# Attention's PSUM banks shared out anew: four for maxima and two for scores, in place of three and three

## The reference, cut to what matters

```
q = (x @ wq_w.T + wq_b).reshape(b, t, H, HD)
k = (x @ wk_w.T + wk_b).reshape(b, t, HKV, HD)
v = (x @ wv_w.T + wv_b).reshape(b, t, HKV, HD)
k1 = k[:, :, 0, :]
v1 = v[:, :, 0, :]
scores = jnp.einsum('bqhd,bkd->bhqk', q, k1) / jnp.sqrt(jnp.float32(HD))
causal = jnp.tril(jnp.ones((t, t), dtype=bool))
scores = jnp.where(causal, scores, -jnp.inf)
weights = jax.nn.softmax(scores, axis=-1)
attn = jnp.einsum('bhqk,bkd->bqhd', weights, v1)
attn = attn.reshape(b, t, H * HD)
return attn @ wo_w.T + wo_b
...
x = _layernorm(x + _L3_attn_ref(x, ...), axis=-1)
```

## Time and profile before

| what | value |
|---|---|
| three executions | 1298.91, 1307.59 and 1310.77 us (median 1307.59) |
| the profiled execution | 1303.14 us, its span 1301.4 us |
| mean granted tensor-engine clock | 0.988 |
| PE busy | 1228.7 us, 94% of the span |
| DVE busy | 719.8 us, 55% |
| ACT busy | 439.8 us, 34% |
| POOL busy | 162.2 us, 12% |
| maxima's reductions on DVE (L2427) | 304, 186.4 us, mean 656 ns |
| exponentials on ACT (L2334) | 288, 156.9 us, mean 603 ns |

### The profile page before, as it was taken

How to read it: one execution, slowest core, us unless ns; L and a number is a source line. 1 busy time by engine, 2 the same in 40 slices (tenths; PEclk the granted TensorE clock), 3 DMA queues, 4 the chain that set the end, 5 groups by cost and what they waited for, 6 DMA issues and landing times. The chain is left out here.

```text
span 1301.4 us, 14425 instructions
## 1 busy us (share of the span) xinstructions
PE 1228.7 (94%) x5396; PEld 846.3 (65%) x5396; DVE 719.8 (55%) x1194; ACT 439.8 (34%) x751; POOL 162.2 (12%) x215
## 2 busy tenths in 40 slices
PE   7899999998998999998889999999999988999998
PEld 4788688644876788876565445455455534788886
DVE  4422565576657656453355678677767734443344
ACT  2121422212211114222333223666565566222221
POOL 0000000000086201002112110011011224000000
PEclk9999999999999999998999999999999998999999
DMA  8110023423045561004000010000000001022001
GB/s 346 33 49 16 33 97 131 169 97 146 1 146 194 206 229 26 22 1 138 1 1 1 5 44 1 2 2 1 2 2 2 3 2 49 25 73 73 1 25 41
DMA packets 18265, 79.07 MB, mean 61 GB/s; under 512 B 3104, under 2 KB 3872, under 8 KB 16032
## 3 DMA queue, kind: packets, MB, share of 16 engines
q1 hardware_dynamic: 18208, 78.32, 16.6%
HBM read 75.95 MB, written 2.10 MB: 60 GB/s over the span
## 5 line engine op out<-in xcount | busy, mean ns | idle before, releaser
L2427 DVE TENSOR_REDUCE mqa_top<-psum 128x1 f32<-128x512 f32 (+3 forms) x304 | 186.4, 656 | 50.6 <-PE psum L2219 25.0
L2334 ACT ACTIVATE mqa_prob<-psum 128x512 f32<-128x512 f32 x288 | 156.9, 603 | 85.2 <-PE psum L2249 81.2
L612 PE MATMUL psum<-L_ffn_x,L_ffn_w_up 128*128 128x512 f32 x624 | 143.8, 391 | 8.7 <-DVE L_ffn_hidden L767 7.7
L612 PEld LDWEIGHTS psum<-L_ffn_x,L_ffn_w_up 128*128 128x128 f32 x624 | 116.5, 188 | 36.0 <-DVE L_ffn_hidden L767 10.2
L612 PE MATMUL psum<-L_attn_x,L_attn_w_up 128*128 128x512 f32 x456 | 105.4, 393 | 3.9 <-DVE L_attn_hidden L767 3.9
L612 PEld LDWEIGHTS psum<-L_attn_x,L_attn_w_up 128*128 128x128 f32 x456 | 86.6, 190 | 22.5 <-issue 4.3
L2249 PE MATMUL psum<-mqa_stack_back,mqa_keys 100*128 100x512 f32 x208 | 96.3, 463 | 0.9 <-DVE mqa_stack_front L2418 0.9
L2262 PE MATMUL psum<-mqa_prob,mqa_v 128*32 128x512 f32 x576 | 78.8, 614 | 0.0
L2156 POOL TENSOR_SCALAR_AFFINE_SELECT mqa_prob<-mqa_prob 128x512 f32<-128x512 f32 x64 | 41.7, 671 | 256.6 <-ACT mqa_prob L2334 256.3
L2249 PEld LDWEIGHTS psum<-mqa_stack_back,mqa_keys 100*128 100x128 f32 x208 | 40.0, 192 | 49.6 <-ACT mqa_prob L2334 42.8
L2219 PE MATMUL psum<-mqa_keys,mqa_stack_back 96*128 96x512 f32 (+1 forms) x160 | 67.2, 442 | 4.0 <-ACT mqa_stack_back L2327 1.5
(11 more groups left out here) (301 smaller groups left out, 2060.0 us busy)
## 6 DMA issues: line engine op xcount, KB each, us to landing
L_ffn_stage<-in_L_w SPq DMA_DIRECT2D x25, 768.0 KB, 4.6
L_ffn_z_int<-in_L_z SPq DMA_DIRECT2D x14, 768.0 KB, 4.2
L_ffn_s_all<-in_L_s SPq DMA_DIRECT2D x14, 768.0 KB, 6.0
heads_wo<-in_L_wo SPq DMA_DIRECT2D x8, 1024.0 KB, 4.8
L_attn_stage<-in_L_w SPq DMA_DIRECT2D x10, 512.0 KB, 3.7
L_attn_w_down<-in_L_down SPq DMA_DIRECT2D x1, 2560.0 KB, 24.1
x_feat<-in_x_feat SPq DMA_DIRECT2D x2, 1024.0 KB, 7.0
x_tok<-in_x_tok SPq DMA_DIRECT2D x1, 2048.0 KB, 18.6
```

Of the source, the lines that this page charges most:

```text
L612: ins = nc.tensor.matmul(bank[place][:, :], w_up[:, slot, w_part, at:at + P], x_half[half][:, x_part, k, :], start=k == 0 and n == 0, stop ...
L2334: nc.scalar.activation(prob[:, n % PROBS, :], score_bank[n % 3], ACT.Exp, scale=SCALE)\
L2427: nc.vector.tensor_reduce(top[:, i % 2, 2 if lo == qt * P else lo // HALF, heads[0]:heads[-1] + 1], max_bank[n % 3][:, 0:len(heads) * widt ...
```

## The change

Scores use two banks, 2 and 3, all the time. Score n waits for n-1 exponentials, which is exponential n-2. Bank 5 goes to the maxima, which rotate through 0, 1, 7 and 5 from the first maximum beyond the first row tile on (n = 72); before that, while bank 5 serves the queries, they rotate through three as before. A maximum beyond the first tile waits for n-3 reductions, and for no fewer than 72, since the rotation starts anew there.

```diff
-        max_bank, score_bank, value_bank = [c.bank[0], c.bank[1], c.bank[7]], [c.bank[2], c.bank[3], c.bank[5]], c.bank[4]
+        score_bank, value_bank = [c.bank[2], c.bank[3]], c.bank[4]
+        first_maxima = sum(e[0] == "max" and e[1] == 0 for e in plan)
+
+        def max_bank(n):
+            beyond = n - first_maxima
+            return c.bank[(0, 1, 7)[n % 3]] if beyond < 0 else c.bank[(0, 1, 7, 5)[beyond % 4]]
+
+        def maxima_taken(n):
+            beyond = n - first_maxima
+            return n - 2 if beyond < 0 else max(first_maxima, n - 3)
+
...
                         if n >= 3:
-                            pe.wait_ge(max_taken, n - 2)
+                            pe.wait_ge(max_taken, maxima_taken(n))
...
-                        out = max_bank[n % 3]
+                        out = max_bank(n)
...
-                        if n >= 3:
-                            pe.wait_ge(exp_ready, n - 2)
+                        if n >= 2:
+                            pe.wait_ge(exp_ready, n - 1)
...
-                        ins = nc.tensor.matmul(score_bank[n % 3], keys[0:SHIFTED, head, cols(kt)],
+                        ins = nc.tensor.matmul(score_bank[n % 2], keys[0:SHIFTED, head, cols(kt)],
```

More of the change, by code:

```diff
@@ L2333, in _ @@
                             act.wait_ge(value_done, n - PROBS + 1)
-                        nc.scalar.activation(prob[:, n % PROBS, :], score_bank[n % 3], ACT.Exp, scale=SCALE)\
+                        nc.scalar.activation(prob[:, n % PROBS, :], score_bank[n % 2], ACT.Exp, scale=SCALE)\
                             .then_inc(exp_ready, 1)
@@ L2428, in _ @@
                                                     heads[0]:heads[-1] + 1],
-                                                max_bank[n % 3][:, 0:len(heads) * width]
+                                                max_bank(n)[:, 0:len(heads) * width]
                                                 .rearrange("p (h k) -> p h k", h=len(heads)), AX.X, ALU.max)\
```

## The result

The changed kernel takes 1314.01 us (median of 20 runs, 1310.43 to 1320.35) against 1305.48 of the kernel before (20 runs, 1296.99 to 1310.77): a ratio of 1.0088, 95% interval 1.007 to 1.0106, which is some 11.5 us more (the two medians alone are 8.5 us apart, the two means 10.5). The forecast was 1321 in a range of 1308 to 1332, and slower by more than 1% as the likeliest case; the sign and the range held, and the loss is a little under 1%.

A forecast was written before the change was run, and what follows sets the result against it. The tensor engine was taken to set the score stage's pace. Terms of 6.6 + 2.8 + 3.0 + 3.9 - 0.5 = 15.8 us gave 1318.9 from the profiled run or 1323.4 from the median; forecast midway 1321 us, range 1308 to 1332.

The forecast's parts named there:

- slower by more than 1%: Whole kernel: the changed kernel takes over 13.1 us longer than before; chance 0.71.
- The mechanism: Scores: score n waits for exponential n-2, with 0.05 us of waking and about 0.10 us for a bare load.
- Term 1: 22 plain groups of four scores, 828.42 to 1001.19 us: each ends 0.30 us late, 6.6 us together.
- Term 2: Six groups from 961 to 973 us with 384-column maxima: fourth score 0.46 us late, 2.8 us together.
- Term 3: Four groups where ScalarE copies a value bank, 1.6 us, and ten others at 0.14 each, 1.4 us; together 3.0 us.
- Masked groups: Groups whose maxima have an extra matmul: third score starts 1.31 us after the first, which covers the wait; no cost.
- Term 4: Last 56 scores, after the last maximum: six plain groups at 0.49 us, 2.9 us; the rest 1.0; together 3.9 us.
- Maxima: Maxima matmuls' waits for VectorE to free a bank: the fourth bank returns 0.5 of 0.8 us.
- The weight loads: Tensor engine queue: if loads were pulled ahead across a semaphore wait, some 11 us instead of 16, about 1314 us.
- The sum: All terms in the score stage: 6.6 + 2.8 + 3.0 + 3.9 - 0.5 = 15.8 us, ends 8.7 and 21.9.
- the rivals' 1314 and 1307 us: 1314: loads pulled ahead across waits; 1307: waits at row-tile ends swallow the loss, 3.9 us left, no change, chance 0.11.
- the rival on it: New gaps lower the tensor engine's clock once in each of eight row tiles: 14 us more, 1335 us, chance 0.08.

The follow-up runs named there:

- The early wait alone: Kernel before with its three score and three maxima banks kept, only score n made to wait for exponential n-2; ratio 1.0084 to the kernel before.
- the kernel with two and three banks: The change without its fourth maxima bank: two score banks, three maxima banks, bank 5 unused; ratio 1.0078 to the kernel before.
- the four banks at the end: Kernel before, with the last 56 scores after the last maximum on four banks instead of three; ratios 0.9985 and 0.9967 to the kernel before.

## Why the prediction was right, and where its sizes were off

- **The mechanism** held in each of its steps: 0.05 us of waking, 0.10 us for a bare load, third and fourth score. The early wait alone makes the whole loss.
- **Term 1**: 3.33 to 3.35 us a group against 3.06 to 3.09, 0.27 instead of 0.30 us; 22 x 0.27 = 5.9 us, not 6.6, since a lead of 0.08 us was enough for the load.
- **Term 2**: 3.27 to 3.29 us a group against 2.83 to 2.87, 0.43 instead of 0.46. The trace has five such groups, not six, so 2.1 us and not 2.8. Its ends, scaled as in term 1, would be 1.6 and 3.4, not 1.8 and 3.0.
- **Term 3**: the four groups with a copy on ScalarE lost 0.41 to 0.44 each, 1.7 us (1.6 predicted). Of the others the two opening groups lost 0.25 and 0.24, the two at either side of the short maxima 0.52 and 0.51 and one 0.12, 1.6 us in all (1.4 predicted), and the rest nothing. Masked groups stayed at 3.99 to 4.01 us, as said.
- **Term 4**: 3 to 3.7 us for 3.9, but not in the parts that it was made of, and so in part by luck. Two groups lost the 0.48 us of a plain one, instead of six; three lost some 0.2, one 0.8, two some 1.5, and one took 1.3 us less.
- **Maxima**: the fourth bank returned nothing where 0.5 us was put. VectorE's row of waits already said that it is the one that waits.
- **The weight loads**: the load is held with its score in each plain group of the changed kernel (848.36 for both); loads let through ahead would have made the loss some 11 us. The Trainium skill (TensorE: Matmul & The Clock Gate, "Architectural detail: the array is 16× 32×32, not 1× 128×128") says that the queue can pull a weight load ahead of matmuls in flight. Across a semaphore wait the trace shows none pulled ahead.
- **The sum**: 15.8 us predicted, 14.5 to 15.1 us in the stage without dips. The terms as measured, 5.9 + 2.1 + 3.3 + 3 to 3.7, are 14.3 to 15.0. Measured in another way, by the starts of the scores in profiles without a dip at that place, all groups up to the last maximum lose 11.4 us together, without two groups of 1012 to 1021 us, where each profile of the change has its dip.
- **The times**: the rivals' 1314 and 1307 us were counted from 1303.14, the forecast's 1321 from a value 2.2 us higher; on that base they would be 1316 and 1309.
- **The clock** is the term that was missing, and the rival on it pointed the wrong way. Over all runs with a clock on record (the first 20 of the kernel before have none) the mean granted clock was 0.9871 before (60 runs) and 0.9893 after (27). At the same clock of 0.991 the means are 1299.2 us (14 runs) and 1312.4 (6), 13.2 us apart; at 0.987 they are 1301.9 (9) and 1316.4 (5), 14.5 apart. The means over all these runs, 1302.65 and 1314.37, are 11.7 apart: some 2 us came back as clock. At equal clock the loss is 1.0 to 1.1%; with the clock it is 0.9%, and so "slower by over 1%", with 0.71, missed while the waits were sized nearly right. That the change itself brought the higher clock is not shown: the kernel with two and three banks has the same score waits and had four dips in the stage.

Here the kernel in whose list the scores' loads wait twice as often for ScalarE (156 times for 75) had the higher mean clock, 0.9893 for 0.9871. The Trainium skill (TensorE: Matmul & The Clock Gate, "A second HAM failure mode: psum-queue depth-cycling") tells of a kernel that cycles through accumulator banks and whose clock swings between its levels from small idle gaps; this case's runs do not show that.

## What to carry to other kernels

How many banks an accumulator's rotation needs is read from one group on the timeline: the time from the matmul to the end of what empties its bank, plus the waking, divided by the pace of the matmuls that use that rotation. In the plain group of the earlier trace rows it is (0.50 + 0.03 + 0.60 + 0.05) / 0.46 = 2.6, with scores 0.46 us apart (841.73 to 842.19), so two banks must stall and three must not, and the list of waits said that maxima had enough. This was tried here with two and three banks where the uses come at an even pace; where they come in bunches, as after the last maximum, the count differs. Where a bank is missing, look first at what could be run between the uses: the same two banks lost 0.27 us a group in one order and 0.03 in another. And where the clock of repeated runs varies, compare them at equal granted clock before a difference of 1% is explained: the four banks at the end looked like a gain of 4 us, of which the banks are shown to give less than one.

## What the runs showed of the hardware that was not expected

- A matmul whose weights start with it, after a wait, took 0.50 us, 0.10 more than with its weights loaded in time; a lead of 0.08 us was already enough to lose only 0.02 (848.85 to 848.93, 0.42 us instead of 0.40).
- PSUM banks that two engines use closely one after the other cost nothing measurable (287.5 us with two score banks and with three).
- The clock's dips came at the same distance from the first score in repeated executions (202 us, three times) though the stage began at different times (828.7, 826.1 and 826.0 us), and a dip cost 1.0 to 1.6 us: 3.3 us for two between profiles of before, 1.5 us for one between profiles of the change, 3.0 us for three between the change and the kernel with two and three banks.
